# A four-layer cross-attention stack: the values' first products in other banks, the last MLP's order, and one MLP's low weight parts moved from VectorE to GpSimd

## The reference, cut to what matters

```python
def layer2(x, ctx, ...):                  # the "third layer"; 0 and 1 are attentions too
    x = attention(layer_norm(x), ctx) + x
    y = gelu(layer_norm(x) @ fc_w + fc_b, approximate=True)     # 256 -> 1024
    return x + y @ proj_w + proj_b                              # 1024 -> 256

def layer3(x, ctx, ctx, ...):             # two cross attentions of 16 heads of 128, then an MLP
    x = x + cross_attention(layer_norm(x), ctx, ...)            # keys/values with one bias row more
    x = x + cross_attention(layer_norm(x), ctx, ...)
    h = gelu(layer_norm(x) @ w_fc1 + b_fc1, approximate=False) @ w_fc2 + b_fc2
    return x + h
```

## Time and profile before

| what | us |
|---|---|
| median of three runs | 992.18 |
| lowest, highest | 990.40, 992.23 |
| profiled execution | 991.19 |
| its span | 989.39 |
| TensorE busy | 953.5 |
| VectorE busy | 737.7 |
| ScalarE busy | 574.4 |
| GpSimd busy | 360.8 |

### The profile page before, as it was taken

The page is one execution under the profiler, slowest core; times in us unless marked ns, Lnnn a source line. Parts: engine busy times, 40 slices in busy tenths (PEclk is TensorE's granted clock), DMA queues, the critical chain, the costliest instruction groups (busy, mean ns, idle before and its releaser), DMA issues.

```text
span 989.4 us, 20036 instructions
## 1 busy us (share of the span) xinstructions
PE 953.5 (96%) x8028; PEld 822.3 (83%) x8028; DVE 737.7 (75%) x1259; ACT 574.4 (58%) x1193; POOL 360.8 (36%) x413
## 2 busy tenths in 40 slices
PE   6999999999998998999999999999999999999997
PEld 5777566556776998998999999999999999889997
DVE  5878999899999788565776677877666766786542
ACT  3557788787876654364545455444544554465552
POOL 2332689898641333011212222431122212282210
PEclk9999999999999999999999999999999999999999
DMA  8302000000000500034233224331222121200001
GB/s 307 106 2 86 1 2 1 2 1 1 2 1 1 204 31 2 1 130 146 74 100 107 84 96 163 108 102 48 86 87 78 51 86 46 83 1 12 23 22 33
DMA packets 31268, 62.30 MB, mean 63 GB/s; under 512 B 4420, under 2 KB 9288, under 8 KB 30536
## 3 DMA queue, kind: packets, MB, share of 16 engines
q1 hardware_dynamic: 31176, 61.02, 18.0%
HBM read 58.91 MB, written 2.10 MB: 62 GB/s over the span
## 4 chain that ended last, share of the span: by engine, by line
PE 80%; DVE 8%; ACT 4%; POOL 4%; issue 4%; DMA 0%; POOLq 0%; DVEq 0%; ACTq 0%
PE work L947 11%; PE work L801 7%; PE work L803 6%; PE work L802 6%; PE work L1060 6%; PE scores L801 6%; PE scores L803 6%; PE scores L802 6%; PE work L1024 5%; PE work L722 3%; PE work L656 3%; PE work L1042 3%; PE work L780 2%; PE work L764 2%; PE work L545 2%
## 5 line engine op out<-in xcount | busy, mean ns | idle before, releaser
L1632 DVE TENSOR_REDUCE smax<-scores 128x16 f32<-128x1024 f32 x32 | 39.2, 1224 | 110.9 <-PE scores L803 110.9
L2179 POOL TENSOR_SCALAR stat<-stat 128x2 f32<-128x2 f32 (+2 forms) x50 | 12.0, 240 | 287.1 <-DVE stat L1206 285.8
L947 PE MATMUL work<-ctxT,w 128*128 128x128 f32 x960 | 112.6, 275 | 0.2 <-DVE all_values L1617 0.2
L947 PEld LDWEIGHTS work<-ctxT,w 128*128 128x128 f32 x960 | 109.9, 192 | 0.8 <-issue 0.8
L2356 POOL TENSOR_TENSOR probs<-probs,smax 128x1024 f32<-128x1024 f32 x22 | 42.2, 1918 | 115.6 <-DVE smax L1657 115.6
L2043 ACT ACTIVATE all_keys<-work 128x512 fp32r<-128x512 f32 x64 | 38.2, 598 | 76.2 <-PE work L1024 76.2
L801 PE MATMUL work<-all_values,pT_l_high 128*128 128x256 f32 x256 | 74.9, 293 | 1.2 <-DVE pT_l_low L1625 1.2
L801 PE MATMUL scores<-all_keys,src_l_high 128*128 128x256 f32 x256 | 74.1, 290 | 0.0
L803 PE MATMUL work<-all_values,pT_l_low 128*128 128x256 f32 x256 | 71.7, 280 | 0.0
L803 PE MATMUL scores<-all_keys,src_l_low 128*128 128x256 f32 x256 | 71.7, 280 | 0.0
L802 PE MATMUL work<-all_values,pT_l_high 128*128 128x256 f32 x256 | 71.6, 280 | 0.0
(11 more groups left out here) (213 smaller groups left out, 3048.1 us busy)
## 6 DMA issues: line engine op xcount, KB each, us to landing
w<-in_l_wk SPq DMA_DIRECT2D x32, 512.0 KB, 4.1
w<-in_l_wv SPq DMA_DIRECT2D x32, 512.0 KB, 5.0
w<-in_l_wq SPq DMA_DIRECT2D x8, 512.0 KB, 5.6
w<-in_l_wo SPq DMA_DIRECT2D x8, 512.0 KB, 5.9
x<-in_x SPq DMA_DIRECT2D x1, 2048.0 KB, 14.5
pair<-in_l_wo SPq DMA_DIRECT2D x4, 512.0 KB, 3.3
out<-x SPq DMA_DIRECT2D x8, 256.0 KB, 2.1
pair<-in_xT SPq DMA_DIRECT2D x1, 1536.0 KB, 8.7
```

The costliest lines, as they stand in the source:

```text
L947: last = mm(bank[:, h * P:(h + 1) * P], w[:, c, h * K3:(h + 1) * K3], ctxT[:, c, p * P:(p + 1) * P], start=(c == 0), stop=(c == DC - 1))
L1632: v.tensor_reduce(m, s3, X, ALU.max).then_inc(d_lmax, 1)
```

## The change

There are three parts.

**The low parts of the third layer's MLP's weights** are made by GpSimd. The eight VectorE subtractions are gone; GpSimd does piece u - 18 at the end of its slot u, for u = 18 to 25.

```diff
-                for q in mlp_pieces(u - 1):          # VectorE
-                    if u != NU - 1:
-                        mlp_weight_low(q)
+                for q in mlp_pieces(u - 1):          # GpSimd, the last thing in a slot
+                    mlp_weight_low(q)
...
+            def mlp_weight_low(q):                   # GpSimd
...
+                g.tensor_tensor(low, mlp_raw[:, w, q * n:(q + 1) * n], high.bitcast(F32), ALU.subtract).then_inc(p_wl, 1)
```

```diff
+        def value_bank(i, q):
+            return fbank[q] if i < 2 else step_banks(i - 2)[2 + q]
...
                 for q in range(2):
-                    if q == 0:
+                    if i < 2:
+                        e.wait_ge(a_lk, 2)
+                        e.wait_ge(d_vl, 2 * (i - 1) + q + 1)
+                    elif q == 0:
                         third_free(j)
                         e.wait_ge(d_kl, 2 * keys_before(j + 1) - 1)
```

```diff
                 if j == 4 * B:
+                    last_norm(2)
                     last_affine(1)
                     hidden_low(0, 0)
...
                 elif j == 4 * B - 1:
                     weight_low(1, 2)
+                    rstd(("m3", 2), TT)
                     weight_low(1, 3)
...
-                if b == 1:
+                if b in (1, B - 1):
                     last_hidden(b, 3)
                 last_projected(b - 1)
-                if b > 1:
+                if 1 < b < B - 1:
                     last_hidden(b, 3)
...
-            mlp_residual(2 * B - 1)
+            for t in range(TT):
+                e.wait_ge(pe_f2, 2 * B + t)
+                e.wait_ge(p_xm, 2 * B)
+                v.tensor_tensor(xb(B - 1)[:, t, :], last_bank(B - 1, t)[:, t * D:(t + 1) * D], xb(B - 1)[:, t, :],
+                                ALU.add).then_inc(d_mr, 1)
```

More of the change, by code:

```diff
@@ L317, in build @@
         d_sum, d_den, d_lrec, d_lr = (sem(f"d_{n}") for n in ("sum", "den", "lrec", "lr"))
-        d_wl, d_sl, d_hl, d_part = (sem(f"d_{n}") for n in ("wl", "sl", "hl", "part"))
+        d_sl, d_hl, d_part = (sem(f"d_{n}") for n in ("sl", "hl", "part"))
         d_kl, d_lh, d_vl, d_tl = (sem(f"d_{n}") for n in ("kl", "lh", "vl", "tl"))
@@ L435, in mlp_bank, with last_bank @@
             return work[3] if b == 0 else work[2 + b % 2]
+        def last_bank(b, t):
+            return work[2] if b == B - 1 and t == 1 else work[b % 2]
         def mlp_pieces(u):
@@ L532, in sync @@
             y = out.rearrange("(n p) d -> p n d", p=P)
-            for b in range(B):
+            for b in range(B - 1):
                 e.wait_ge(d_mr, B + b + 1)
                 nc.sync.dma_start(y[:, TT * b:TT * (b + 1), :], xb(b)).then_inc(s_out, 16)
-            e.wait_ge(s_out, 16 * B)
+            for t in range(TT):
+                i = TT * (B - 1) + t
+                e.wait_ge(d_mr, 2 * B + t)
+                nc.sync.dma_start(y[:, i:i + 1, :], x[:, i:i + 1, :]).then_inc(s_out, 16)
+            e.wait_ge(s_out, 16 * (B - 1 + TT))
         def tensor(e):
@@ L821, in hidden @@
                 e.wait_ge(a_wh, 4)
-                e.wait_ge(d_wl, 4)
+                e.wait_ge(p_wl, 4)
                 if b > 0:
@@ L837, in projected @@
                 e.wait_ge(a_wh, 8)
-                e.wait_ge(d_wl, 8)
+                e.wait_ge(p_wl, 8)
                 if b < 2:
@@ L922, in tensor @@
                         queries(u + 1)
+                if u == NU - 1:
+                    mlp_source(0)
                 if tiles:
                     probs_transposed(tiles[0])
-                if u == NU - 1:
-                    mlp_source(0)
                 if u > 0:
@@ L1000, in tile_scores @@
                     e.wait_ge(a_g, 4 * B)
+                    e.wait_ge(d_vl, 4)
                 else:
@@ L1056, in value_products @@
                         e.wait_ge(d_kl, 2 * keys_before(j + 1))
-                    bank = step_banks(j)[2 + q]
+                    bank = value_bank(i, q)
                     for bb in range(2):
@@ L1107, in last_hidden @@
                 e.wait_ge(a_wh, 8 + 4)
-                e.wait_ge(p_wl, 4)
+                e.wait_ge(p_wl, 8 + 4)
                 if b > 0:
@@ L1123, in last_projected @@
                 e.wait_ge(a_wh, 16)
-                e.wait_ge(p_wl, 8)
+                e.wait_ge(p_wl, 16)
                 if b < 2:
@@ L1132, in last_projected @@
                     for f in range(FC):
-                        last = products(work[b % 2][:, t * D:(t + 1) * D],
+                        last = products(last_bank(b, t)[:, t * D:(t + 1) * D],
                                         [v[:, f, t * P:(t + 1) * P] for v in hid_parts[b % 2]],
                                         [w[:, f, :] for w in w2_parts], f == 0, f == FC - 1)
-                last.then_inc(pe_f2, 1)
+                    if t == TT - 1 or b == B - 1:
+                        last.then_inc(pe_f2, 1)
             for i in range(2):
@@ L1369, in mlp_norm @@
                 ln_finish(("m2", b), xb(b), norm[(B + b) % 3], TT)
-            def mlp_weight_low(q):
-                w, q = divmod(q, 4)
-                n = mlp_raw.shape[2] // 4
-                high, low = (flat(v)[:, q * n:(q + 1) * n] for v in (m2_w1, m2_w2)[w])
-                e.wait_ge(a_wh, 4 * w + q + 1)
-                v.tensor_tensor(low, mlp_raw[:, w, q * n:(q + 1) * n], high.bitcast(F32), ALU.subtract).then_inc(d_wl, 1)
             def mlp_affine(b):
@@ L1761, in vector @@
                 if b + 2 < B:
-                    last_norm(b + 2)
+                    if b > 0:
+                        last_norm(b + 2)
                     last_normal(b + 2)
@@ L2252, in mlp_bias @@
                 add_row(b, "l2_pb", p_xm)
+            def mlp_weight_low(q):
+                w, q = divmod(q, 4)
+                n = mlp_raw.shape[2] // 4
+                high, low = (flat(v)[:, q * n:(q + 1) * n] for v in (m2_w1, m2_w2)[w])
+                e.wait_ge(a_wh, 4 * w + q + 1)
+                g.tensor_tensor(low, mlp_raw[:, w, q * n:(q + 1) * n], high.bitcast(F32), ALU.subtract).then_inc(p_wl, 1)
             g.memset(minus_half[:, :], -0.5).then_inc(p_const, 1)
```

7 lines of the change are left out of this document (3 added, 4 removed).

## The result

The changed kernel takes 986.41 us (median of four runs, 986.17 to 986.76) against 991.68 for the kernel before on the same chip: ratio 0.9948, 95% interval 0.9932 to 0.9964, that is 5.3 us faster. The profiled execution took 986.49, its span 984.7.

The account below looks back on a forecast made before the run. TensorE, busy 953.5 of 989.4 us, was taken as the bound. Terms 0.3 - 1.5 - 0.5 - 0.9 - 0.7 = -3.3 us gave 987.9 against the profiled 991.2, 988.9 against the median; range 986.8 to 991.4.

Parts of the forecast that it names:

- Rival 5: Granted clock: without the half-clock stretch a run lands near 987.2, with a second near 990.6; chances 0.09 and 0.10.
- D: End of last MLP, TensorE's order of batch 7: residual and last low part come earlier, -0.9 us.
- A: Low parts on GpSimd, slots 18 to 25: saves 1.6 us, holds VectorE's normalisations 1.9; +0.3, between -1.6 and +1.0.
- Rival 1: Slots 21 and 22: GpSimd's pieces do not hold the normalisations; low parts give -1.6, total 987.0; chance 0.17.
- the prediction's strict reading: Slot 25: source low part, with two SBUF inputs, runs under a pushed-back GpSimd addition, up to 1.3 us more.
- B: Steps -2 and -1, banks of first value products: both 0.75 us waits go, -1.5 us, between -1.9 and 0.
- Rival 2: Bank edit only moves the wait to the next step's products: between -0.75 and 0, about 990.4; chance 0.12.
- C: Last MLP's start, batch 2's statistics earlier: -0.9 wait, +0.4 hold; -0.5 us, between -1.5 and +0.3.
- A gap above 1 us: Sign of error: such a gap between batches 0 and 1 of the last MLP would make the statistics edit a loss.
- Rival 3: Batch 7's wait ahead of the last projection vanishes whole: -2.4 us, total 987.4; chance 0.03.
- E: Kernel's end, last batch in halves: shorter last addition and store, -0.7 us, between -0.3 and -0.9.
- Rival 4: All six pieces in slots 18 to 23 hold VectorE by 1.3 us each: +6.2, total 994.8; chance 0.04.

Follow-up runs that it names:

- D alone: Kernel before with only TensorE's order of batch 7's last hidden piece and batch 6's projection changed: 988.89 us, ratio 0.9970.
- the full change without D: Changed kernel with TensorE's order of batch 7's last hidden piece and batch 6's projection as before: 988.83 us, ratio 0.9977.
- A alone: Kernel before with only the low parts on GpSimd and slot 23's four transposes ahead of the eight: 990.86 us, ratio 0.9993.
- the two pieces put back: Changed kernel, but VectorE makes low-part pieces 3 and 4 (slots 21 and 22) as before, GpSimd the other six: 986.36 us.
- the later additions: Changed kernel, but GpSimd begins the last MLP's bias additions only behind batch 2's normalisation: 985.56 us.
- B alone: Kernel before with only the banks of the first two value quarters' products changed: 988.84 us, ratio 0.9974.
- the low part early: Changed kernel, with VectorE's last low part ahead of the query-weight sums in the third MLP's batches 2 to 5: 984.49 us, ratio 0.9926.

## Why the prediction was off, point by point

- **The clock, the step that failed.** Rival 5 made it a matter of luck, "a run without it" or "one with a second", and carried the forecast over to the median by adding the 0.99 between profile and median. That took for granted that the changed kernel has the same stretches as the kernel before. It has not. At equal clock the change gives 988.8 - 986.3 = 2.5 us; the other 2.8 of the 5.3 are stretches at half clock, two in most runs of before, one in a third of the runs after. One of them hangs on D: it lies behind the very wait that D shortens. D alone moves the median by 3.3 and not by 0.9, and the full change without D loses 2.3. The other, at 401 us, still falls in some runs after; in the first profile it fell at 387 us, where the next wait covered it. The sum of the edits alone was off on the other side, 2.5 us at equal clock for 3.3 forecast, most of it by A.
- **What stood in the profile and was not used.** The stretch at 0.93 in the earlier trace rows begins 1.4 us behind a wait of TensorE of 1.8 us; the only longer one from 300 us on, 2.36 us, is the one that D edits. I had priced the half clock (1.75, measured 1.5) but had not asked which wait it follows.
- **A: right in mechanism, too low in size.** +0.3 forecast, between -1.6 and +1.0; measured 0.8 to 0.86 in the traces, 1.4 alone and 1.0 out of the full change at clock 1.000. The holds were nearly as forecast (2.08 - 1.12 = 0.96 and 1.80 - 0.73 = 1.07, for 0.95 each). The saving was 1.5 for 1.6: the pair of slot 21 starts 0.45 us earlier in A alone (292.70 for 293.15), and 0.51 comes back behind each of the two holds. What the sum lacked is 0.3 us in slot 23: the hold of slot 22 makes TensorE's scores late, and VectorE waits for them. Rival 1 (no hold) is out by the two pieces put back. By the traces A would gain about 0.5 with the other six alone on GpSimd; the runs at clock 1.000, 985.4 and 985.3, do not show it. The Trainium skill's page GPSIMD Engine Reference, section Key points, says that GpSimd shares its SBUF interfaces with VectorE, with contention for instructions in a 2-port mode or with two SBUF inputs. The trace agrees for the low parts with two SBUF inputs (1.77 and 2.51 us for 0.69), and the sums (one input, 1.21 us) kept their length. The normalisations, with one input, were held too; whether they run in a 2-port mode no trace says. The source's low part of slot 25, for which the prediction's strict reading allowed 1.3 us, took 1.02 us for 0.69, and TensorE's shift did not move there.
- **B: right.** -1.5 forecast, -1.63 in both pairs of traces. Rival 2 is out: the remaining wait in these steps (0.6 us, one time) was there before.
- **C: right.** -0.5 forecast, -0.58 and -0.55 measured, with the parts larger than mine: the earlier hold and the old wait gone, 1.7, a new wait of 1.0 to 1.2. I had put that new wait at 0.4. A gap above 1 us was to be the sign of a loss; it came (1.03), and C was a gain all the same. Without it C is worth 1.3 more, as the later additions showed.
- **D's own term: right.** -0.9 forecast, -0.93 in the trace, low part behind the residual as forecast. Rival 3's -2.4 needed VectorE's order to change; with that order changed it came.
- **E: right.** -0.7 forecast, -0.7 in the trace, about -0.6 at clock 1.000 (one run).
- **Rival 4** (all pieces hold) is out: by the traces six of the eight cost nothing. The row that the prediction named against it was ill chosen: at 287.85 us GpSimd stood idle (from 285.1 to 289.5), so it showed nothing about a sum beside GpSimd. The sum at 264.90 us above does.
- **The chances** of "faster" add up to 0.79 and not 0.78; nothing hangs on it.

The traces' sum of the five is -3.0 for -3.3 forecast, and the runs at clock 1.000 say -2.5.

What stays open: why a given run of one kernel has the stretch and the next has not, though the waits are the same; and why A alone and B alone had few runs with two (2 of 12 and 1 of 10, before 18 of 33 beside them), though their wait ahead of the last projection is the 2.36 us of before.

## What to carry to other kernels

Where the page shows the granted clock below 1.00 for a stretch, look for TensorE's wait just ahead of it, and list all other waits of that length: an edit that shortens one of them can be worth, beside its own length, the matmuls that the half clock costs behind it. Compare kernels at equal mean clock before adding up parts, and report the median apart. Here a GpSimd instruction of 1.3 to 2.4 us held VectorE's normalisations and its instructions with two SBUF inputs (0.73 us became 1.80, 0.69 became 2.5). Where a signal of VectorE starts it, it meets what stands next in VectorE's list, so put there one that nobody waits for.

## What the runs showed of the hardware that I had not expected

- In the twenty profiles the clock fell eighteen times, apart from the last microseconds of a program, and at few places: at 387 us in three profiles (a wait of 1.75), around 401 us in nine (1.8), at 977 to 981 us in three (2.36), at 419 to 422 us in two (2.2), and for 6.8 us around the wait of 5.0. Except for this last one it fell between 0.05 us before and 1.5 us after the end of the wait. The waits of 1.4 us at 373 us, of 1.4 to 1.7 at 315 us and of 1.43 ahead of the last projection had none behind them in any profile. The two kernels whose longest wait in the third MLP was 1.0 us had none in nine runs; the other kernels with D's order and the waits of 1.4 to 1.8 us had clock 1.000 in 24 of 49.
- A stretch costs 1.5 us where matmuls fill it (31 for 44 in 5 us), and nothing where a wait for another engine follows within some 10 us (387 us, and the wait at 400). That would explain why runs of equal clock differ (before at 0.998 took from 988.75 to 991.6); the place of the stretch in the faster ones was not seen.
- Removing a wait of TensorE can leave the engine it waited for with the same queue: with the low part early VectorE's held instruction only moved, and 4.9 us of waits gave 1.6.
- The hold works the other way too: a bias addition on GpSimd (128x512), 1.28 us long at 302.63 in the full change, took 2.81 us at 382.66 with the low part early, beside VectorE's two-input instructions.
